# Two first expert tiles of a routed feed-forward layer moved in front of the loop and of the expert table

## Chip, cores and metric

The kernel runs on one core of one Trainium2 chip. The metric is device time in microseconds (us) of one execution. Engines are named as the profile names them: PE (TensorE), DVE (VectorE), ACT (ScalarE), POOL (GpSimd), SP (SyncE, which here only issues DMAs); PEld is the weight load of PE, and a name with a q at its end is the sequencer of that engine.

## What is computed

One transformer block on 1024 tokens of width 256: a normalised attention layer with 16 heads (softmax attention mixed with a linear-attention term), and then a feed-forward layer with 8 experts, of which each token takes its best 2. The second part is the one touched here:

```python
B, S, H, F, E, K = (2, 128, 256, 688, 8, 2)
logits = xf @ router_w.T
top_v, top_i = jax.lax.top_k(logits, K)
probs = jax.nn.softmax(top_v, axis=-1)
combine = jnp.sum(jax.nn.one_hot(top_i, E) * probs[..., None], axis=1)
g = jnp.einsum('th,efh->etf', xf, gate_w)
u = jnp.einsum('th,efh->etf', xf, up_w)
y = jnp.einsum('etf,ehf->eth', jax.nn.silu(g) * u, down_w)
out = jnp.einsum('te,eth->th', combine, y)
```

## The kernel before

Attention is worked off in 256 steps; work on the first half of the tokens (projection, norm, router, slots) is dealt out between its last steps. The experts are not computed for all tokens. Every token row, with its weight and number, is scattered to DRAM (`xg_d`, one list of rows for each expert): POOL does this with 8 indirect DMAs for each half of the tokens (`scatter`, L518 to L525; semaphore `scattered`). A tile is 128 rows of one list. The experts of the two first tiles (`EARLY = 2`) come from the counts of the first half alone (`early_ready`); those of all others from a table that DVE works out once the second half is routed (L975 to L1005, semaphore `expert_ready`, 2 at its end). The table also gives the number of pairs of tiles (`pairs`) and whether one is left over (`left`); each engine reads both into registers and runs a loop over pairs.

One tile t, with its buffers of parity t % 2, goes through these steps:

- SP: `load_xg` (L418) reads the row from a table into a register and brings 128 rows from `xg_d`.
- PE: `turn_x` (L1288) transposes the rows to bank 7 of PSUM; DVE: `xgT_copy` (L948) copies them and the two words of meta data.
- PE: `gate_up` (L1283), 16 matmul instructions to banks 0 to 3; ACT: `silu` (L646), reads banks 0 and 1; DVE: `hidden` (L1008), multiplies with banks 2 and 3.
- PE: `turn_hidden` (L1318), 6 transposes to banks 4 and 5; DVE: `hidT_copy` (L1014), two copies.
- PE: `down` (L1325), 12 matmul instructions to bank 6; ACT: `weigh` (L651), scales by the row's weight; POOL: `add_y` (L545), an indirect DMA that adds the rows to `sum_d`. DVE's `take_meta` (L1025) copies the meta data for `weigh` and `add_y`, and waits for the `add_y` of two tiles before.

In the loop body PE has the order: gate_up(t), turn_x for t+1, down(t-1), turn_hidden(t), gate_up(t+1), turn_x for t+2, down(t), turn_hidden(t+1), with t = 2i+1; this run has 20 tiles. Each engine takes its instructions in the order written; engines meet in semaphores alone.

Ahead of the loop, PE computes gate_up of tile 0 in pieces between the routing of the second half (L1309 to L1315). Then every engine waits for `expert_ready`, reads `pairs` and `left`, and only then goes on: DVE with `hidden(0, 0)`, PE with `turn_hidden(0, 0)` and the first pair of the loop (tiles 1 and 2), SP with the rows of tiles 2 and 3. SP waits for `scattered[1]` before `expert_ready`.

A load of a register from memory is `value_load`; on PE it is `load_expert` (L1272) for an expert's number. L1048 is the helper through which all matmuls pass, so a row of L1048 is told by its place and its count.

Of the kernel before, what the change touches and what calls it, by code (L numbers as in the profile page):

```python
# [13 lines left out]
P = 128  # L14
# [5 lines left out]
FB = [P, P, P, P, 88, 88]  # L20
FO = [sum(FB[:i]) for i in range(len(FB))]
FN = F // 2
NTILE = (K * T + E * (P - 1)) // P
EARLY = 2
PAIRS = (EARLY + NTILE - 1) // 2
# [47 lines left out]
def block_kernel(nc, x_d, w_d, rope_d, const_d, gate_d, router_d, gu_d, dn_d, out_d):  # L73
    ctx = ExitStack()
    with ctx:
# [120 lines left out]
        meta = keep(2, 2, dt=U32)  # L196
# [149 lines left out]
        def _(sp):  # L346
# [65 lines left out]
            def start_sum(hf):  # L412

                sp.wait_ge(x2_ready, 2 * hf + 2)
                sp.dma_start(sum_d[hf * HALF:(hf + 1) * HALF].rearrange("(n p) h -> p n h", p=P),
                             x[:, 4 * hf:4 * hf + 4]).then_inc(sum_init, 16)
# [11 lines left out]
            for t in range(EARLY):  # L428
                load_xg(t, t)
            start_sum(1)  # L430
            sp.wait_ge(scattered[1], 16 * K * 4)
            sp.wait_ge(expert_ready, 2)
            pairs = sp.value_load(pairs_i[0:1, 0:1], min_val=1, max_val=PAIRS)
            left = sp.value_load(pairs_i[0:1, 1:2], min_val=0, max_val=1)
            with sp.Fori(0, PAIRS) as i:
                with sp.If_lt(sp.to_reg(i), pairs):
                    for r in (1, 2):
                        t = 2 * i + r
                        sp.wait_ge(xgT_ready, t)
                        load_xg(t + 1, (r + 1) % 2)  # L440
# [7 lines left out]
        def _(pool):  # L448
# [93 lines left out]


            pool.wait_ge(sum_init, 48)
            def add_y(t, par):  # L545
                pool.wait_ge(y_added, 16 * t)
                pool.wait_ge(y_ready, t + 1)
                pool.sem_inc(y_taken, 1)
                pool.indirect_dma_start(  # L549
                    out=sum_d, out_offset=bass.IndirectOffsetOnAxis(ap=meta_y[:, par, 1:2], axis=0),  # L550
                    in_=yt[:, par], in_offset=None, compute_op=ALU.add).then_inc(y_added, 16)

            pool.wait_ge(expert_ready, 2)
            pairs = pool.value_load(pairs_i[0:1, 0:1], min_val=1, max_val=PAIRS)
            left = pool.value_load(pairs_i[0:1, 1:2], min_val=0, max_val=1)
            with pool.Fori(0, PAIRS) as i:
                with pool.If_lt(pool.to_reg(i), pairs):
                    for r in (0, 1):
                        add_y(2 * i + r, r)
# [6 lines left out]
        def _(act):  # L566
# [79 lines left out]
            def silu(t, par):  # L646
                act.wait_ge(gu_ps, t + 1)
                nc.scalar.activation(act_g[:, par].rearrange("p (b c) -> p b c", b=2),  # L648
                                     psum[:, 0:2, 0:FN], ACT.Silu).then_inc(silu_ready, 1)
# [5 lines left out]
                                     scale=meta_y[:, par, 0:1].bitcast(F32)).then_inc(y_ready, 1)  # L655

            silu(0, 0)
            act.wait_ge(expert_ready, 2)
            pairs = act.value_load(pairs_i[0:1, 0:1], min_val=1, max_val=PAIRS)
            left = act.value_load(pairs_i[0:1, 1:2], min_val=0, max_val=1)  # L660
            with act.Fori(0, PAIRS) as i:
                with act.If_lt(act.to_reg(i), pairs):
                    for r in (1, 2):
                        t = 2 * i + r
                        silu(t, r % 2)
                        act.wait_ge(y_added, 32 * i)
                        weigh(t - 1, (r + 1) % 2)
# [9 lines left out]
        def _(dve):  # L677
# [3 lines left out]
            def link(ins):  # L681

                chain[0] += 1
                ins.then_inc(dve_step, 1)
                dve.wait_ge(dve_step, chain[0])
# [230 lines left out]
            def steps(i, t):  # L916
# [8 lines left out]
                if isinstance(n, int) and n in SIDE:  # L925
# [19 lines left out]
                    if f == "early":  # L945
                        (early_counts, early_taken, early_experts)[k]()

            def xgT_copy(t, par):  # L948
                dve.wait_ge(xgT_ps, t + 1)
                V.tensor_copy(meta[:, par], xg[:, par, H:ROW].bitcast(U32))  # L950
                V.tensor_copy(xgT[:, par], psum[:, 7, 0:HB * P].rearrange("p (b c) -> p b c", b=HB)).then_inc(xgT_ready, 1)
# [12 lines left out]
            for k in range(K):  # L964
                for n in range(4):
# [7 lines left out]


            link(V.tensor_copy(cnt, psum[:, 4, 0:E]))  # L975
            link(V.tensor_tensor(cmp, cnt.unsqueeze(2).to_broadcast([P, E, E]),
                                 const[:, C_J:C_J + E * E].rearrange("p (e j) -> p e j", e=E), ALU.is_gt))
            link(V.tensor_reduce(tiles, cmp, AX.X, ALU.add))
# [15 lines left out]

            link(V.tensor_tensor(tau, cum.unsqueeze(1).to_broadcast([P, NTILE + 1, E]),
                                 const[:, C_TAU:].rearrange("p (n e) -> p n e", e=E), ALU.is_le))
            V.tensor_reduce(ex_f, tau, AX.X, ALU.add)
# [5 lines left out]
            V.tensor_scalar(row_i[:, EARLY:], ex_r, float(P), float(E * T), ALU.mult, ALU.min).then_inc(expert_ready, 1)  # L1005


            def hidden(t, par):  # L1008
                dve.wait_ge(silu_ready, t + 1)
                V.tensor_tensor(hid[:, par].rearrange("p (b c) -> p b c", b=2),  # L1010
                                act_g[:, par].rearrange("p (b c) -> p b c", b=2),
                                psum[:, 2:4, 0:FN], ALU.mult).then_inc(hid_ready, 1)

            def hidT_copy(t, par):  # L1014
                dve.wait_ge(hidT_ps, t + 1)
                V.tensor_copy(hidT[:, par, 0:4], psum[:, 4].rearrange("p (c t) -> p c t", c=4))  # L1016
                V.tensor_copy(hidT[0:FB[4], par, 4:6], psum[0:FB[4], 5, 0:2 * P].rearrange("p (c t) -> p c t", c=2)
                              ).then_inc(hidT_ready, 1)

            dve.wait_ge(expert_ready, 2)  # L1020
            pairs = dve.value_load(pairs_i[0:1, 0:1], min_val=1, max_val=PAIRS)
            left = dve.value_load(pairs_i[0:1, 1:2], min_val=0, max_val=1)
            hidden(0, 0)
            hidT_copy(0, 0)
            def take_meta(t, par):  # L1025

                dve.wait_ge(y_added, 16 * (t - 1))
                dve.wait_ge(xgT_ready, t + 1)
                V.tensor_copy(meta_y[:, par], meta[:, par])  # L1029

            with dve.Fori(0, PAIRS) as i:
                with dve.If_lt(dve.to_reg(i), pairs):
                    for r in (1, 2):
                        t = 2 * i + r
                        take_meta(t, r % 2)
                        xgT_copy(t + 1, (r + 1) % 2)
                        hidden(t, r % 2)
                        hidT_copy(t, r % 2)
# [7 lines left out]
        def _(pe):  # L1046
# [225 lines left out]
            def load_expert(t):  # L1272
                return pe.value_load(ex_i[0:1, bass.ts(t, 1)], min_val=0, max_val=E - 1)
# [9 lines left out]
            def gate_up(t, par, e):  # L1283
                pe.wait_ge(xgT_ready, t + 1)
                pe.wait_ge(hid_ready, t)
                columns(par, e, range(4)).then_inc(gu_ps, 1)

            def turn_x(par, loads):  # L1288
                pe.wait_ge(xg_in[par], 16 * loads)
                for b in range(HB):  # L1290
                    ins = nc.tensor.transpose(psum[:, 7, b * P:(b + 1) * P], xg[:, par, b * P:(b + 1) * P], ident)  # L1291
                ins.then_inc(xgT_ps, 1)
# [25 lines left out]
            def turn_hidden(t, par):  # L1318
                pe.wait_ge(hid_ready, t + 1)
                for c, (o, n) in enumerate(zip(FO, FB)):  # L1320
                    ins = nc.tensor.transpose(psum[0:n, 4 + c // 4, (c % 4) * P:(c % 4 + 1) * P],  # L1321
                                              hid[:, par, o:o + n], ident)
                ins.then_inc(hidT_ps, 1)

            def down(t, par, e):  # L1325
                pe.wait_ge(hidT_ready, t + 1)
                pe.wait_ge(y_ready, t)
                for c, n in enumerate(FB):
                    ins = mm(psum[:, 6, 0:H], hidT[0:n, par, c], dn[0:n, c, e], start=(c == 0),
                             stop=(c == len(FB) - 1))  # L1330
                ins.then_inc(y_ps, 1)

            pe.wait_ge(expert_ready, 2)
            pairs = pe.value_load(pairs_i[0:1, 0:1], min_val=1, max_val=PAIRS)
            left = pe.value_load(pairs_i[0:1, 1:2], min_val=0, max_val=1)
            turn_hidden(0, 0)
            pe.wait_ge(gu_in, 16 * E)
            pe.wait_ge(dn_in, 16 * len(FB))
            with pe.Fori(0, PAIRS) as i:
                with pe.If_lt(pe.to_reg(i), pairs):  # L1340

                    t = 2 * i + 1
                    e1 = load_expert(t)
                    gate_up(t, 1, e1)
                    turn_x(0, i + 2)
                    down(t - 1, 0, load_expert(t - 1))
                    e2 = load_expert(t + 1)
                    turn_hidden(t, 1)
                    gate_up(t + 1, 0, e2)
                    turn_x(1, i + 2)  # L1350
                    down(t, 1, e1)
                    turn_hidden(t + 1, 0)
# [35 lines left out]
```

## Time and profile before

| | us |
|---|---|
| median of 3 runs | 513.32 (511.92 to 514.02) |
| the profiled execution | 510.48 |
| its span in the trace | 508.6 |
| mean granted clock of PE | 0.927 |
| PE busy | 434.0 |
| DVE busy | 282.3 |
| ACT busy | 194.4 |
| POOL busy | 100.2 |

The first row of a timeline view gives: start in us from the beginning of the span, busy time, engine, line, operation, shapes, number of instructions, and in brackets the idle time before it with what ended it. The chain of waits follows the work that ended last backwards through what released it; "issue" in it is time in which nothing visible was waited for. [...] Ends of matmuls are modelled, so neighbouring rows can overlap by some tenths.

### The profile page before, as it was taken

The page shows a single profiled execution, that of the slowest core. Times are in us where ns is not written, and L with a number is a line of the kernel's source. Part 1 is how long each engine was busy: PE and PEld are TensorE (multiplying, and loading weights), DVE is VectorE, ACT ScalarE, POOL GpSimd, SP SyncE. Part 2 cuts the span into 40 slices and gives each one's busy share as a digit, 9 for nine tenths or more (in the row PEclk, how much of TensorE's full clock was granted, in tenths as well). Part 3 has the DMA queues.
Part 4 walks back from the last instruction along what each step waited for, and adds up shares of the span by engine and source line. Part 5 has one row for each costly group of instructions (what it writes and reads, how often), then busy time and mean ns, then how long its engine had stood idle before and what let it go on. Part 6 is the DMA issues. An engine that isn't in the chain of part 4 may idle for free.

```text
span 508.6 us, 7202 instructions
## 1 busy us (share of the span) xinstructions
PE 434.0 (85%) x2056; PEld 225.2 (44%) x2057; DVE 282.3 (56%) x511; ACT 194.4 (38%) x341; POOL 100.2 (20%) x91
## 2 busy tenths in 40 slices
PE   0990696898999999999998978589999999999981
PEld 0560263222222222424222335357777777777751
DVE  6577689587878887698884116512323323232310
ACT  1136410576676767575667941001111111110100
POOL 6252430111111110010060021602112121212111
PEclk9996597799999999999899997589999999999987
DMA  6137674194939361000021159412121212212004
GB/s 214 66 104 155 130 121 111 51 286 153 309 122 306 121 205 31 0 2 0 2 74 54 33 203 294 176 38 32 31 31 31 31 32 31 40 31 31 10 12 103
DMA packets 24452, 48.42 MB, mean 95 GB/s; under 512 B 4240, under 2 KB 17808, under 8 KB 22576
## 3 DMA queue, kind: packets, MB, share of 16 engines
q0 software_dynamic: 7824, 30.23, 20.7%
q1 hardware_dynamic: 16032, 16.35, 12.7%
q10 hardware_dynamic: 576, 1.58, 1.0%
q8 instruction: 11, 0.18, 0.2%
q14 instruction: 9, 0.07, 0.0%
HBM read 30.44 MB, written 18.70 MB: 97 GB/s over the span
## 4 chain that ended last, share of the span: by engine, by line
PE 66%; DVE 9%; DMA 9%; SPq 5%; issue 4%; ACT 3%; POOL 2%; POOLq 1%; DVEq 0%; ACTq 0%
PE psum L1048 61%; DMA mem<-parts_d 3%; DVE mem L755 3%; PE psum L1321 2%; DMA parts_d<-mem 2%; SPq L372 2%; ACT mem L628 2%; SPq L367 2%; DMA mem<-mem 1%; DMA mem<-x 1%; SPq L380 1%; PE psum L1291 1%; PE psum L1168 1%; DVE mem L845 1%; DMA xg_d<-mem 1%
## 5 line engine op out<-in xcount | busy, mean ns | idle before, releaser
L1048 PE MATMUL psum<-mem 128*32 128x512 f32 (+11 forms) x1800 | 406.7, 468 | 39.1 <-DMA mem<-parts_d 15.7
L1048 PEld LDWEIGHTS psum<-mem 128*128 128x128 f32 (+7 forms) x1800 | 192.6, 144 | 228.9 <-issue 98.1
L755 DVE TENSOR_REDUCE mem<-psum 128x1 f32<-128x1024 f32 x128 | 152.9, 1219 | 37.7 <-PE psum L1048 35.6
L628 ACT ACTIVATE mem<-psum 128x512 f32<-128x512 f32 x256 | 138.0, 605 | 88.8 <-PE psum L1048 86.1
L549 POOL DMA_INDIRECT sum_d<-mem x20 | 31.1, 1554 | 139.9 <-ACT mem L654 133.1
L648 ACT ACTIVATE mem<-psum 128x688 f32<-128x688 f32 x20 | 14.9, 743 | 107.9 <-PE psum L1048 107.9
L1029 DVE COPY mem<-mem 128x2 uint32<-128x2 uint32 x19 | 3.2, 169 | 62.8 <-DMA sum_d<-mem 62.8
L1016 DVE COPY mem<-psum 128x512 f32<-128x512 f32 x20 | 13.8, 692 | 38.7 <-PE psum L1321 37.1
L654 ACT ACTIVATE mem<-psum,mem 128x256 f32<-128x256 f32 x20 | 9.5, 473 | 48.3 <-PE psum L1048 48.3
L499 POOL DMA_DIRECT2D xg_d<-mem x9 | 8.1, 898 | 86.8 <-PE psum L1048 86.8
L1321 PE MATMUL psum<-mem 128*128 128x128 f32 (+1 forms) x120 | 17.3, 282 | 5.4 <-DVE mem L1010 5.4
L1010 DVE TENSOR_TENSOR mem<-mem,psum 128x688 f32<-128x688 f32 x20 | 17.4, 870 | 7.4 <-ACT mem L648 4.6
L1321 PEld LDWEIGHTS psum<-mem 128*128 128x128 f32 (+1 forms) x120 | 14.7, 141 | 8.6 <-DVE mem L1010 6.4
L523 POOL DMA_INDIRECT xg_d<-mem x16 | 15.8, 985 | 7.8 <-issue 4.2
L811 DVE RECIPROCAL mem<-psum 128x16 f32<-128x16 f32 x8 | 2.1, 258 | 26.9 <-PE psum L1168 26.7
L1055 PE MATMUL psum<-mem 128*128 128x128 f32 x16 | 3.9, 426 | 13.0 <-DVE mem L697 13.0
L459 POOL TENSOR_TENSOR mem<-mem 128x2 f32<-128x2 f32 (+1 forms) x6 | 5.2, 864 | 43.2 <-DVE mem L692 43.2
L484 POOL COPY mem<-mem 128x512 f32<-128x512 f32 x8 | 4.8, 611 | 39.9 <-PE psum L1048 39.9
L478 POOL TENSOR_TENSOR mem<-mem 128x2048 f32<-128x2048 f32 x2 | 9.0, 4507 | 13.8 <-ACT mem L598 7.9
L950 DVE COPY mem<-mem 128x2 uint32<-128x2 uint32 x20 | 3.4, 170 | 13.6 <-PE psum L1291 13.6
L469 POOL TENSOR_TENSOR mem<-mem 128x512 f32<-128x512 f32 x4 | 6.9, 1722 | 17.5 <-DVE mem L743 17.5
L731 DVE TENSOR_TENSOR mem<-mem 128x1024 bf16<-128x1024 f32 x4 | 7.1, 1774 | 4.4 <-ACT mem L587 4.4
(120 smaller groups left out, 191.6 us busy)
## 6 DMA issues: line engine op xcount, KB each, us to landing
mem<-gate_up POOLq DMA_DIRECT2D x8, 1376.0 KB, 8.4
xg_d<-mem POOLq DMA_DIRECT2D x8, 1032.0 KB, 6.8
mem<-down POOLq DMA_DIRECT2D x4, 1024.0 KB, 8.0
parts_d<-mem SPq DMA_DIRECT2D x12, 256.0 KB, 2.5
mem<-parts_d SPq DMA_DIRECT2D x24, 128.0 KB, 4.2
mem<-parts_d SPq DMA_DIRECT2D x48, 64.0 KB, 2.2
mem<-xg_d SPq DMA_DIRECT2D x20, 129.0 KB, 2.0
mem<-down POOLq DMA_DIRECT2D x2, 704.0 KB, 15.3
```

The lines of the kernel that those rows point to most:

```text
L367: sp.dma_start(kst[g * HD:(g + 1) * HD, qd], src).then_inc(done, 16)
L372: sp.dma_start(qst[g * HD:(g + 1) * HD, sl], src[:, :, cols(hf)]).then_inc(q_in, 16)
L523: pool.indirect_dma_start(out=xg_d, out_offset=bass.IndirectOffsetOnAxis(ap=slot[:, hf, k, n:n + 1], axis=0), in_=xn2[:, n, k], in_offset= ...
L549: pool.indirect_dma_start(out=sum_d, out_offset=bass.IndirectOffsetOnAxis(ap=meta_y[:, par, 1:2], axis=0), in_=yt[:, par], in_offset=None, ...
L628: nc.scalar.activation(prob[:, t % 8], psum[:, score_bank(n, t)], ACT.Exp, scale=HD ** -0.5).then_inc(exp_ready, 1)
L648: nc.scalar.activation(act_g[:, par].rearrange("p (b c) -> p b c", b=2), psum[:, 0:2, 0:FN], ACT.Silu).then_inc(silu_ready, 1)
L654: nc.scalar.activation(yt[:, par], psum[:, 6, 0:H], ACT.Copy, scale=meta_y[:, par, 0:1].bitcast(F32)).then_inc(y_ready, 1)
L755: V.tensor_reduce(mx[:, par, k:k + 1], banks(2 * (k % 2), 2), AX.X, ALU.max).then_inc(max_ready, 1)
L1010: V.tensor_tensor(hid[:, par].rearrange("p (b c) -> p b c", b=2), act_g[:, par].rearrange("p (b c) -> p b c", b=2), psum[:, 2:4, 0:FN], AL ...
L1016: V.tensor_copy(hidT[:, par, 0:4], psum[:, 4].rearrange("p (c t) -> p c t", c=4))
L1048: return nc.tensor.matmul(*a, **k)
L1321: ins = nc.tensor.transpose(psum[0:n, 4 + c // 4, (c % 4) * P:(c % 4 + 1) * P], hid[:, par, o:o + n], ident)
```

## The change

The pair of tiles 1 and 2 is written out in front of the loop, which now starts at pair 1, on every engine. Tiles 0 and 1 are finished without the table:

- DVE: `hidden(0, 0)` stands right behind the copy of the counts (L975), ahead of the table; `hidT_copy(0, 0)` in the middle of it (behind L992). `hidden`, `take_meta` and `hidT_copy` of tile 1 follow the table, and only then come the wait for it and the two register loads. The functions `hidden`, `hidT_copy` and `take_meta` are moved up as they are.
- PE: turn_hidden(0), gate_up(1), down(0), turn_hidden(1), down(1) come ahead of the wait for the table; then the loads of `pairs`, `left` and the third expert, turn_x for tile 2, gate_up(2), turn_x for tile 3, turn_hidden(2).
- ACT: both silu and both weigh ahead of the wait; silu(2) behind it.
- POOL: the two first add_y ahead of the wait.
- SP: waits for the table first and for `scattered[1]` second, issues the rows of tiles 2 and 3, and loads `pairs` and `left` after that.

```diff
             start_sum(1)
+            sp.wait_ge(expert_ready, 2)
             sp.wait_ge(scattered[1], 16 * K * 4)
-            sp.wait_ge(expert_ready, 2)
+            for t in range(EARLY):
+                sp.wait_ge(xgT_ready, t + 1)
+                load_xg(EARLY + t, t)
             pairs = sp.value_load(pairs_i[0:1, 0:1], min_val=1, max_val=PAIRS)
             left = sp.value_load(pairs_i[0:1, 1:2], min_val=0, max_val=1)
-            with sp.Fori(0, PAIRS) as i:
+            with sp.Fori(1, PAIRS) as i:
...
-            def add_y(t, par):
-                pool.wait_ge(y_added, 16 * t)
+            def add_y(t, par, first=False):
+                if not first:
+                    pool.wait_ge(y_added, 16 * t)
...
+            add_y(0, 0, first=True)
+            add_y(1, 1)
             pool.wait_ge(expert_ready, 2)
...
             silu(0, 0)
+            silu(1, 1)
+            weigh(0, 0)
+            weigh(1, 1)
             act.wait_ge(expert_ready, 2)
             pairs = act.value_load(pairs_i[0:1, 0:1], min_val=1, max_val=PAIRS)
             left = act.value_load(pairs_i[0:1, 1:2], min_val=0, max_val=1)
-            with act.Fori(0, PAIRS) as i:
+            silu(2, 0)
+            with act.Fori(1, PAIRS) as i:
...
             link(V.tensor_copy(cnt, psum[:, 4, 0:E]))
+            hidden(0, 0)
             link(V.tensor_tensor(cmp, cnt.unsqueeze(2).to_broadcast([P, E, E]),
...
+            hidT_copy(0, 0)
             link(V.tensor_tensor(tau, cum.unsqueeze(1).to_broadcast([P, NTILE + 1, E]),
...
+            hidden(1, 1)
+            take_meta(1, 1, first=True)
+            hidT_copy(1, 1)
             dve.wait_ge(expert_ready, 2)
             pairs = dve.value_load(pairs_i[0:1, 0:1], min_val=1, max_val=PAIRS)
             left = dve.value_load(pairs_i[0:1, 1:2], min_val=0, max_val=1)
-            hidden(0, 0)
-            hidT_copy(0, 0)
...
-            with dve.Fori(0, PAIRS) as i:
+            xgT_copy(2, 0)
+            take_meta(2, 0)
+            xgT_copy(3, 1)
+            hidden(2, 0)
+            hidT_copy(2, 0)
+            with dve.Fori(1, PAIRS) as i:
...
+            e1 = load_expert(1)
+            turn_hidden(0, 0)
+            gate_up(1, 1, e1)
+            pe.wait_ge(dn_in, 16 * len(FB))
+            down(0, 0, e0, first=True)
+            turn_hidden(1, 1)
+            down(1, 1, e1)
             pe.wait_ge(expert_ready, 2)
             pairs = pe.value_load(pairs_i[0:1, 0:1], min_val=1, max_val=PAIRS)
             left = pe.value_load(pairs_i[0:1, 1:2], min_val=0, max_val=1)
-            turn_hidden(0, 0)
+            e2 = load_expert(2)
+            turn_x(0, 2)
             pe.wait_ge(gu_in, 16 * E)
-            pe.wait_ge(dn_in, 16 * len(FB))
-            with pe.Fori(0, PAIRS) as i:
+            gate_up(2, 0, e2)
+            turn_x(1, 2)
+            turn_hidden(2, 0)
+            with pe.Fori(1, PAIRS) as i:
```

## Rows read from the trace of the kernel before

**Rows 1.** The page: PE's granted clock in 40 equal slices; shares of the chain.

```profile
PEclk9996597799999999999899997589999999999987
PE 66%; DVE 9%; DMA 9%; SPq 5%; issue 4%; ACT 3%; POOL 2%; POOLq 1%; DVEq 0%; ACTq 0%
```

**Rows 2.** Chain of waits, 323 to 360 us: start, duration, what.

```profile
328.99 3.26 DMA xg_d<-mem
332.27 0.27 SPq L433
...
334.52 1.96 DMA mem<-xg_d
...
355.74 0.22 PE psum L1291 x2
355.96 2.59 PE psum L1048 x12
358.55 0.66 PE psum L1321 x6
359.21 4.63 PE psum L1048 x16
```

**Rows 3.** Timeline of PE, 282 to 352 us (columns as told above).

```profile
313.35 7.76 PE L1048 MATMUL psum<-mem 128*128 128x8 f32 x40 [0.73 <-ACT mem L612]
326.55 1.54 PE L1321 MATMUL psum<-mem 128*128 128x128 f32 x6 [5.43 <-DVE mem L1010]
328.09 6.70 PE L1048 MATMUL psum<-mem 128*128 x16
336.53 0.44 PE L1291 MATMUL psum<-mem 128*128 128x128 f32 x2 [1.73 <-DMA mem<-xg_d]
337.51 4.44 PE L1048 MATMUL psum<-mem 128*128 x12 [0.55 <-issue]
...
350.85 1.42 PE L1048 MATMUL psum<-mem 128*128 x4
```

**Rows 4.** Timeline of DVE, ACT and POOL, 282 to 352 us.

```profile
319.55 0.16 DVE L975 COPY mem<-psum 128x8 f32<-128x8 f32 x1
...
323.66 0.18 DVE L1005 TENSOR_SCALAR mem<-mem 128x24 int32<-128x24 f32 x1
325.62 0.87 DVE L1010 TENSOR_TENSOR mem<-mem,psum 128x688 f32<-128x688 f32 x1 [1.78 <-issue]
...
337.08 0.42 DVE L951 COPY mem<-psum 128x256 f32<-128x256 f32 x1
...
342.75 0.69 DVE L1016 COPY mem<-psum 128x512 f32<-128x512 f32 x1 [4.47 <-PE psum L1321]
343.35 0.41 DVE L1017 COPY mem<-psum 88x256 f32<-88x256 f32 x1
347.19 0.17 DVE L1029 COPY mem<-mem 128x2 uint32<-128x2 uint32 x1 [3.43 <-DMA sum_d<-mem]
...
321.15 0.74 ACT L648 ACTIVATE mem<-psum 128x688 f32<-128x688 f32 x1 [3.06 <-PE psum L1048]
...
341.99 0.47 ACT L654 ACTIVATE mem<-psum,mem 128x256 f32<-128x256 f32 x1 [6.42 <-PE psum L1048]
```

**Rows 5.** PE over chosen stretches: us, busy (instructions), granted clock, DMA share, GB/s.

```profile
310.00:312.00 2.00, 0.47 (x4) 1.00 0.92 225
328.10:331.70 3.60, 3.60 (x7) 0.50 0.30 100
338.80:341.60 2.80, 2.80 (x8) 0.50 0.18 47
342.40:350.80 8.40, 8.40 (x39) 1.00 0.21 32
```

**Rows 6.** POOL's scatter of the second half, first and last of 8.

```profile
319.94 1.06 POOL L523 DMA_INDIRECT xg_d<-mem  x1 [3.30 <-DVE mem L892]
...
328.99 0.96 POOL L523 DMA_INDIRECT xg_d<-mem  x1 [0.30 <-issue]
```

More of the change, by code:

```diff
@@ L555, in _ @@
             left = pool.value_load(pairs_i[0:1, 1:2], min_val=0, max_val=1)
-            with pool.Fori(0, PAIRS) as i:
+            with pool.Fori(1, PAIRS) as i:
                 with pool.If_lt(pool.to_reg(i), pairs):
@@ L946, in steps, with hidden, hidT_copy, take_meta @@
                         (early_counts, early_taken, early_experts)[k]()
+            def hidden(t, par):
+                dve.wait_ge(silu_ready, t + 1)
+                V.tensor_tensor(hid[:, par].rearrange("p (b c) -> p b c", b=2),
+                                act_g[:, par].rearrange("p (b c) -> p b c", b=2),
+                                psum[:, 2:4, 0:FN], ALU.mult).then_inc(hid_ready, 1)
+            def hidT_copy(t, par):
+                dve.wait_ge(hidT_ps, t + 1)
+                V.tensor_copy(hidT[:, par, 0:4], psum[:, 4].rearrange("p (c t) -> p c t", c=4))
+                V.tensor_copy(hidT[0:FB[4], par, 4:6], psum[0:FB[4], 5, 0:2 * P].rearrange("p (c t) -> p c t", c=2)
+                              ).then_inc(hidT_ready, 1)
+            def take_meta(t, par, first=False):
+                if not first:
+                    dve.wait_ge(y_added, 16 * (t - 1))
+                dve.wait_ge(xgT_ready, t + 1)
+                V.tensor_copy(meta_y[:, par], meta[:, par])
             def xgT_copy(t, par):
@@ L1005, in _ @@
             V.tensor_scalar(row_i[:, EARLY:], ex_r, float(P), float(E * T), ALU.mult, ALU.min).then_inc(expert_ready, 1)
[L1008 to L1018, printed above, removed]
+            hidden(1, 1)
+            take_meta(1, 1, first=True)
+            hidT_copy(1, 1)
             dve.wait_ge(expert_ready, 2)
@@ L1022, in _ @@
             left = dve.value_load(pairs_i[0:1, 1:2], min_val=0, max_val=1)
-            hidden(0, 0)
-            hidT_copy(0, 0)
[L1025 to L1029, printed above, removed]
-            with dve.Fori(0, PAIRS) as i:
+            xgT_copy(2, 0)
[4 more added lines that the diff above has]
+            with dve.Fori(1, PAIRS) as i:
                 with dve.If_lt(dve.to_reg(i), pairs):
@@ L1323, in turn_hidden, with down @@
                 ins.then_inc(hidT_ps, 1)
-            def down(t, par, e):
+            def down(t, par, e, first=False):
                 pe.wait_ge(hidT_ready, t + 1)
-                pe.wait_ge(y_ready, t)
+                if not first:
+                    pe.wait_ge(y_ready, t)
                 for c, n in enumerate(FB):
```

## The prediction

> **What bounds the kernel now.** I read the page first. Its chain of waits is 66% PE, and the clock row has two dips of PE, one early and one shortly after the middle of the run, at slices 25 to 27 [rows 1]. That second dip is where the change works, so I then went through the chain from 320 us on, and beside it the timelines of all engines. From 350.85 us on PE has no gap: one tile takes 0.22 + 2.59 + 0.66 + 4.63 = 8.10 us, and matmul follows matmul [rows 2]. The stretch in front of it is different. PE ends its columns of tile 0 at 313.35 + 7.76 = 321.11 us, then stands for 5.43 us, works at half clock, stands for 1.73 us until the rows of tile 2 arrive, stands for 0.55 us for a register load, and only at 350.85 us begins the gate_up of tile 3 [rows 3]. Between 321.11 and 350.85 us lie 29.7 us, and the work in them (three turn_hidden, two gate_up, two turn_x, two down) costs at full clock 3 x 0.66 + 2 x 4.63 + 2 x 0.22 + 2 x 2.59 = 16.9 us. So 12.9 us are lost: 5.43 + 1.73 + 0.55 = 7.7 us idle and the rest, 5.2 us, mostly in the half clock.
>
> Why PE stands: `hidden(0, 0)` on DVE begins at 325.62, though its silu is over at 321.15 + 0.74 = 321.89 us. DVE is on the table until 323.84 and then spends 1.78 us on the wait and the two register loads [rows 4]. The chain itself runs elsewhere: over the last scatter (328.99 + 3.26 = 332.25 us), SP's registers and the rows of tile 2, which leave at 334.52 and are there at 336.48 us [rows 2]. Before, PE's first gap is therefore partly free: had PE been earlier with gate_up(1) alone, it would have waited longer for tile 2. The change moves both: the DVE work, and down(0), turn_hidden(1) and down(1) ahead of tile 2, so that PE has work while the scatter lands.
>
> **The new order, step by step,** in the times of the profiled execution; all up to 321.89 us stays.
>
> DVE waits behind the counts (319.55 + 0.16 = 319.71) for silu(0), which ends at 321.89. hidden(0) costs 0.87 and ends at 322.82 with the hand-over (0.06, as 325.62 + 0.87 = 326.49 against 326.55). Queued behind that wait is the table: it took 323.84 - 319.71 = 4.13 us, and with hidT_copy(0) in it (0.69 and 0.41 in a row, 343.76 - 342.75 = 1.01 us) it now ends at 322.82 + 4.13 + 1.01 = 327.96 instead of 323.84 us [rows 4]. Who waits for it: SP, which has to wait for the scatter till 332.25 anyway [rows 2], POOL and ACT, which take their first tiles ahead of it, and PE, not before 335. So 4.1 us of delay are free, with 4.3 us to spare; the cover is the scatter, and without it the table would cost its whole delay.
>
> PE: turn_hidden(0) from 322.88. At half clock it takes 1.54 us as before, to 324.42; gate_up(1) 6.70 us as before, to 331.12 [rows 3]. These two prices depend on when the clock returns. Before, it returned some 5.3 us after PE had restarted (half clock in 328.1 to 331.7, full from 332 on); in 338.8 to 341.6 the half clock lasted only about 3.4 us in all [rows 5]. With the same 5.3 us I take 6.70; the return 2 us earlier or 1.5 us later moves the end by 1.0 us down or 0.8 us up. down(0) needs hidT_copy(0), which lies inside a table that ends at 327.96, long before 331.12, and its weights, for which no wait shows before. It costs 2.59 [rows 2], to 333.71. Before, the same down took 4.44 us because the clock had fallen again [rows 3, 5]; here no gap precedes it. Meanwhile silu(1) 0.74 and hidden(1) 0.87 end at 331.12 + 0.74 + 0.87 + 0.1 = 332.83, so turn_hidden(1), 0.66, follows at once, to 334.37. hidT_copy(1), 1.05 with its hand-over, leaves PE idle to 335.45; that wait is new, since in the loop a gate_up covers it. down(1) 2.59, to 338.04.
>
> Behind down(1) in PE's sequencer stand three register loads. One left 0.55 us visible on PE [rows 3], two took 1.78 with the wait on DVE [rows 4]: three cost 1.65 to 2.67 us, beside a down of 2.59 us that also has to be issued. Exposed are 0 to 1.0 us; I take 0.35, nearer PE's own row. So turn_x(2) begins at 338.4. Its rows: SP now loads only the row's register after 332.25. Before, three loads and the loop's start took 334.52 - 332.27 = 2.25 us [rows 2]; one of three is some 0.75, so the DMA leaves at 333.0 and lands 1.96 later, at 335.0. That DMA moves 1.5 us forward and still counts for nothing: 3.4 us of slack. turn_x(2) 0.44, xgT_copy 0.42 and hand-overs (337.08 + 0.42 - 336.97 = 0.53 from the end of turn_x, [rows 3, 4]): gate_up(2) starts at 339.4 and ends at 344.0, turn_x(3) at 344.25. take_meta(2) waits for the first add_y: before, it came at 347.19, 4.73 us after weigh ended at 342.46 [rows 4]; now weigh(0) ends at about 334.3, so it is there at 339.0, before DVE wants it. The two register loads of DVE (1.78) lie between 336.5 and 338.3, under down(1).
>
> Then the price of peeling: turn_hidden(2) has no down in front of it as in the loop. silu 0.74 + hidden 0.87 + hand-overs put it at 345.8, an idle stretch of 1.5 us. It releases the sequencer too, which then enters the loop and loads a register before gate_up(3): before, this lasted from 326.55 to 328.09, 1.54 us [rows 3], against 0.66 of turn_hidden at full clock. So gate_up(3) starts at 347.35. Before it was 350.85 [rows 3]. **Sum: 350.85 - 347.35 = 3.5 us.** By parts: idle falls from 7.7 to 1.7 + 1.1 + 0.35 + 0.5 + 1.5 + 0.9 = 6.05 us, 1.65 less, and the fall of the clock around down(0) goes, 4.44 - 2.59 = 1.85 us. After it loop, skipped turns and tail are the same, each shifted by this; add_y takes 4.7 us a tile against 8.1 us of PE, so it doesn't bind. Below these bounds nothing: no work is taken out but one wait.
>
> POOL's issues of the scatter were 1.06 us beside the table and 0.96 us without [rows 6]. More copies of DVE now run beside them; eight times 0.1 is 0.8 us at most, under the slack of 3.4 us. [...]
>
> **The rivals.**
> A, the sum above: -3.5 us.
> B, the clock falls once more. PE's new gaps of 1.5 and 0.9 us at 344.25 to 347.35, with 0.7 us of work between, resemble the 1.73 and 0.55 us after which the clock fell before [rows 3, 5]; speaking against it, a gap of 1.5 us (PE busy 0.47 of 2.00) at 310 us left the clock at 1.00 [rows 5]. Price: as for down(0), 1.85 us, so -1.65 us, 511.7. [...]
> C, the clock is back earlier than before: gate_up(1) at 4.63 instead of 6.70 us. PE then stands only 1.7 us instead of 5.43 before turn_hidden(0), which speaks for it; that it was at half clock already before that gap speaks against it [rows 1]. -5.5 us, 507.8.
> D, the transfers are the bound: the change moves nothing of the scatter, and if tile 2 lands later than 338.4 the gain shrinks by the excess. It would take 3.4 us more of scatter; from 6.9 us more nothing is left. At 5 us of delay: -1.9 us, 511.4.
> E, slower: the short gaps at 334.4, 338.0 and 344.3 us each cost a fall of the clock, so PE never runs warm till the loop. Three times 1.85 is 5.55 us, from the second on the gain is about gone (-3.5 + 3.7): +2.05 us, 515.4.
>
> **How the numbers follow.** The profiled execution took 510.48 us, 1.9 more than its span; the sum makes it 507.0. The median of the runs shown is 513.32, and even the lowest is 1.4 above the profiled one. The difference of the two kernels is what I work out, so it goes off the median: 513.32 - 3.5 = 509.8. Chances: A 0.58, B 0.19, C 0.12, D 0.04, E 0.07. A's own range, with gate_up(1) -1.0 to +0.8, the registers -0.35 to +0.65 and 0.7 us of scatter between medians (511.92 to 514.02 for single runs), is 507.8 to 511.9. To leave out no more than 2 in 10 it must take in B and most of C: 507.3 to 512.4. A measurement of this kernel can tell about 0.5%, 2.6 us, from no change; that bound is at 510.75. C and most of A lie below it, B, D and the weak end of A within: faster 0.65, same 0.30, slower 0.05.
>
> **What would show it.** In the profile after: hidden(0) at about 321.95 and PE's gap ahead of turn_hidden(0) 1.7 us; the table's end at 328; down(0) right behind gate_up(1), 12 instructions in 2.6 us; a gap of about 1.1 us before down(1); rows of tile 2 landed at 335, and no wait of turn_x(2) for a DMA; gaps of 1.5 and 0.9 us around turn_hidden(2); the gate_up of tile 3, 16 instructions, from 347.35. Wrong would be: turn_x(2) waiting for the DMA (D), PEclk of 0.5 after 345 (B) or 1.00 already at 325 (C), a stretch at 0.50 behind each gap (E), or a tail longer than before, which no step above foresees.

## The result, and the profile after

The changed kernel takes 507.36 us at the median of 20 runs, the kernel before 513.27 at the median of 20. The ratio is 0.9883 with a 95% interval of 0.9858 to 0.9909: 6.0 us faster (4.7 to 7.3), where 3.5 were forecast. Two more measurements of the same pair gave 0.9908 (0.9882 to 0.9934) and 0.9900 (0.9865 to 0.9935). The forecast of 509.8 us was 2.4 us too slow, and the first ratio stands at the very end of the range (513.32 x 0.9883 = 507.3).

The profiled execution of the changed kernel took 508.72 us, its span is 506.9 (508.6 before), mean granted clock 0.932 as a share of full speed (so 1.00 is full and 0.50 half clock in what follows; PEclk on the page is in tenths). The page has its second dip of the clock at slices 25 to 27 like [rows 1], but shallower, and it reaches into slice 28:

```profile
PEclk9996587599999999999998998788999999999997
PE 67%; DVE 11%; DMA 7%; SPq 5%; issue 4%; ACT 3%; POOL 1%; POOLq 0%; DVEq 0%; ACTq 0%
```

The timeline of PE from 290 to 352 us answers to [rows 3]. L1067 is the helper of the matmuls, L1340 turn_hidden, L1310 turn_x; in each variant below these lines have other numbers by a few, so tell a row by its place and its count:

```profile
314.88 8.00 PE L1067 MATMUL psum<-mem 128*128 128x8 f32 x40 [0.73 <-ACT mem L618]
324.69 0.87 PE L1340 MATMUL psum<-mem 128*128 128x128 f32 x6 [1.81 <-DVE mem L960]
325.40 7.38 PE L1067 MATMUL psum<-mem 128*128 x28
332.72 0.88 PE L1340 MATMUL psum<-mem 128*128 128x128 f32 x6
335.18 4.54 PE L1067 MATMUL psum<-mem 128*128 x12 [1.59 <-DVE mem L967]
339.56 0.38 PE L1310 MATMUL psum<-mem 128*128 128x128 f32 x2
340.68 4.89 PE L1067 MATMUL psum<-mem 128*128 x16 [0.74 <-issue]
...
347.31 0.87 PE L1340 MATMUL psum<-mem 128*128 128x128 f32 x6 [1.52 <-DVE mem L960]
348.78 3.90 PE L1067 MATMUL psum<-mem 128*128 x7 [0.60 <-issue]
```

The order is the one forecast: a gap of 1.81 us instead of 5.43, gate_up(1) and down(0) in one row of 28 instructions, the new waits ahead of down(1) and turn_hidden(2). One thing is not: turn_hidden(0) takes 0.87 us and not 1.54, and the 28 instructions take 7.38 us and not 6.70 + 2.59 = 9.29. PE is at full clock here (1.00 in 322 to 335 us). In this execution part of that is lost again, since the clock falls in down(1) (0.50 in 336 to 339 us, 4.54 us for 12 instructions).

This execution reached the end of tile 0's columns 1.8 us later than that of before (322.88 against 321.11), from what came earlier, which the change doesn't touch. So the fair measure is the stretch from there to the gate_up of tile 3: 348.78 - 322.88 = 25.9 us, before 29.7. Behind it both are equally long: 506.9 - 348.8 = 158.1 us, before 157.8. That is partly chance in this trace: the first gate_up of the loop runs at half clock for a while (0.50 in 349.4 to 352.6 us, 6.58 us in all instead of 4.89), and in return the fall of the clock that the kernel before has near its end (0.50 in 486 to 488 us) is missing.

### The profile page after: what moved, and what is told of

Its sections match the earlier page's. It is cut to its first block, busy times and chain, and to the rows that moved or that the text cites. A ratio compares the mean times of both kernels' runs of the same rounds, so it can differ in the third digit from the quotient of the medians.

```text
span 506.9 us, 7154 instructions
## 1 busy us (share of the span) xinstructions
PE 434.5 (86%) x2056; PEld 226.3 (45%) x2057; DVE 282.0 (56%) x511; ACT 194.8 (38%) x341; POOL 100.2 (20%) x91
## 4 chain that ended last, share of the span: by engine, by line
PE 67%; DVE 11%; DMA 7%; SPq 5%; issue 4%; ACT 3%; POOL 1%; POOLq 0%; DVEq 0%; ACTq 0%
PE psum L1067 62%; DVE mem L765 4%; DMA mem<-parts_d 3%; PE psum L1340 3%; DMA parts_d<-mem 2%; SPq L372 2%; ACT mem L634 2%; SPq L367 2%; DMA mem<-x 1%; PE psum L1187 1%; PE psum L1310 1%; DVE mem L855 1%; DVE mem L738 1%; POOL mem L462 1%; DVE mem L741 0%
## 5 line engine op out<-in xcount | busy, mean ns | idle before, releaser
L1067 PE MATMUL psum<-mem 128*32 128x512 f32 (+11 forms) x1800 | 407.6, 469 | 39.9 <-DMA mem<-parts_d 15.2
L1067 PEld LDWEIGHTS psum<-mem 128*128 128x128 f32 (+7 forms) x1800 | 194.2, 144 | 229.7 <-issue 99.9
L975 DVE COPY mem<-mem 128x2 uint32<-128x2 uint32 x19 | 3.2, 168 | 55.8 <-DMA sum_d<-mem 55.7
L1340 PE MATMUL psum<-mem 128*128 128x128 f32 (+1 forms) x120 | 16.6, 274 | 3.3 <-DVE mem L960 3.3
L1340 PEld LDWEIGHTS psum<-mem 128*128 128x128 f32 (+1 forms) x120 | 13.8, 135 | 6.2 <-DVE mem L960 4.5
L481 POOL TENSOR_TENSOR mem<-mem 128x2048 f32<-128x2048 f32 x2 | 9.0, 4508 | 13.3 <-ACT mem L604 7.9
```

The source lines that it names most:

```text
L1067: return nc.tensor.matmul(*a, **k)
```

## The experiments

Each was timed in rounds against the kernel before on the same chip; "stretch" is the time from the end of tile 0's columns to the gate_up of tile 3 in its own trace.

**The kernel before, again (before_again).** No edit.

> The kernel before, unchanged, timed against itself, to see how far its executions spread and where the granted clock of PE falls in another execution. Theory 'clock' (the new order by itself is worth the 3.5 to 3.8 us of the sum, and the other 2 us of the measured 5.9 come from fewer falls of PE's clock on average): ratio 1.00 within 0.3%; the half-clock stretches around 325 to 342 us and at the tail (485 us) sit elsewhere or are missing in this profile, and the span from the end of the columns of tile 0 to the gate_up of tile 3 differs from 29.7 us by up to 2 us. Theory 'size' (a step of the sum is mis-sized, the clock is the same on average): that span is 29.7 us within 0.3 us again.

Measured: 0.9992 (0.997 to 1.0013); stretch 30.3 us. Mean granted clock over 25 executions of the kernel before 0.9305. The clock around the stretch, as views of PE over windows (us, busy, granted clock, DMA share, GB/s):

```profile
318.00:322.00 4.00, 3.98 (x22) 0.50 0.96 341
322.50:325.50 3.00, 0.00 (x0) 1.00 0.35 128
326.00:332.40 6.40, 4.97 (x12) 0.50 0.30 105
```

Here the clock had come back at 322.3 us, while PE stood in its gap of 5.43 us, and was gone again when turn_hidden(0) began at 327.41. In the first trace it was at half clock all through the gap. To PE it makes no difference: in both traces gate_up(1) begins at half clock behind this gap. Neither theory got what it asked for: the half-clock stretches sit where they sat (gate_up(1) 6.64, down(0) 4.54 us), against 'clock', and the stretch differs from 29.7 by 0.6 us, against 'size'.

**The changed kernel, again (after_again).** No edit.

> The changed kernel again. Both theories: ratio 0.988 within 0.003 to the kernel before. Theory 'clock': mean granted clock over its executions is 0.008 to 0.015 above that of the kernel before (2 us lost less are 4 us less at half clock, and 17 us fewer in the stretch around the two first tiles), and the span from the end of the columns of tile 0 to the gate_up of tile 3 varies by 1 us or more between this profile and the first (25.9 us). Theory 'size': that span is 25.9 us within 0.3 us again, and the mean clocks differ by under 0.004.

Measured: 0.9908 (0.9882 to 0.9934); mean clock 0.942 over 6 executions (0.940 over the 20 of the first measurement): 0.010 to 0.012 above the kernel before, as theory 'clock' had it. Stretch 25.2 us, 0.7 from the first: between the two theories.

```profile
312.00:318.00 6.00, 6.00 (x36) 0.50 0.51 147
318.50:322.00 3.50, 1.69 (x11) 1.00 0.68 283
322.00:331.00 9.00, 7.97 (x35) 1.00 0.30 105
```

The clock comes back ahead of the gap, and it is still at 1.00 behind the 1.81 us of idle. Something new stands in the chain of waits:

```profile
328.29 2.86 DMA xg_d<-mem
...
331.92 3.37 DMA mem<-xg_d
335.29 0.04 issue
335.33 0.44 PE psum L1310 x2
```

PE, now early, waits 1.29 us for the rows of tile 2, and their load takes 3.37 us where it took 1.96 [rows 2]. POOL had issued the first add_y 1.27 us before this load:

```profile
330.65 1.62 POOL L553 DMA_INDIRECT sum_d<-mem  x1 [1.39 <-issue]
```

**SP's part alone (sp_first).** The kernel before with:

```diff
+            sp.wait_ge(expert_ready, 2)
             sp.wait_ge(scattered[1], 16 * K * 4)
-            sp.wait_ge(expert_ready, 2)
+            for t in range(EARLY):
+                sp.wait_ge(xgT_ready, t + 1)
+                load_xg(EARLY + t, t)
...
-            with sp.Fori(0, PAIRS) as i:
+            with sp.Fori(1, PAIRS) as i:
```

> The kernel before with SP's part of the change alone: the rows of tiles 2 and 3 leave before pairs and left are loaded. Theory 'clock': they land 1.5 us earlier, PE's gap before turn_x(2) shrinks from 1.73 to about 0.2 us, and with a gap that short the clock does not fall in down(0): -1.5 us, or -3.3 us where the fall would have come. Rival 'all needed together' (nothing of the change is worth anything while the first hidden waits for the table): 0 within 0.5 us. From my sum: -1.5 to -3.3 us.

Measured: 0.9955 (0.9934 to 0.9977), 2.3 us faster; stretch 26.6 us, 3.4 less than the mean of the three traces of before.

```profile
328.21 6.47 PE L1051 MATMUL psum<-mem 128*128 x16
335.22 0.44 PE L1294 MATMUL psum<-mem 128*128 128x128 f32 x2 [0.54 <-DMA mem<-xg_d]
336.21 2.85 PE L1051 MATMUL psum<-mem 128*128 x12 [0.55 <-issue]
```

The load left 0.8 us after the scatter had landed instead of 2.25, so 1.5 us sooner; the wait is 0.54 instead of 1.73 us, and down(0) keeps its clock (1.00 in 332 to 340 us): 2.85 against 4.44 us [rows 2, 3]. In the trace this is worth more than the 1.5 us, since down(0), behind the shorter wait, keeps its clock; the measured gain, 1.2 to 3.4 us by its interval, doesn't decide between 1.5 us alone and the two together.

**Down(1) behind gate_up(2) (order2).** The changed kernel with:

```diff
-            down(1, 1, e1)
             pe.wait_ge(expert_ready, 2)
...
             gate_up(2, 0, e2)
             turn_x(1, 2)
+            down(1, 1, e1)
             turn_hidden(2, 0)
```

and weigh(1) behind silu(2), DVE's register loads ahead of hidden(1).

> The changed kernel with down(1) moved behind gate_up(2) and turn_x(3), as in the loop (weigh(1) behind silu(2), and DVE's two register loads ahead of hidden(1)). If the peeled order costs what the sum says (1.1 us idle before down(1), 0.35 of register loads, 1.5 idle before turn_hidden(2) and 0.9 behind it, less a wait of about 1.1 us for tile 2's rows and their copy), the gate_up of tile 3 starts 3.1 us earlier than in the changed kernel: -3.1 us to it, -9 us to the kernel before (ratio 0.982). Rival: the new gap of 1.7 us at 334.4 makes the clock fall in gate_up(2), which costs 1.9 us: -1.2 us to the changed kernel.

Measured: 0.9945 (0.9923 to 0.9966), some 2 us slower than the changed kernel, where 3.1 faster was expected; stretch 28.2 us.

```profile
331.32 0.82 PE L1340 MATMUL psum<-mem 128*128 128x128 f32 x6
337.49 0.69 PE L1310 MATMUL psum<-mem 128*128 128x128 f32 x2 [5.36 <-DMA mem<-xg_d]
338.92 7.53 PE L1067 MATMUL psum<-mem 128*128 x16 [0.74 <-issue]
```

PE is done with turn_hidden(1) 10.6 us after the columns (the sum had 13.3), the rows come at 15.9, and with nothing in between the gap grows to 5.36 us and gate_up(2) runs at half clock (0.50 in 334.2 to 344 us), as the rival had it, but behind a gap three times as long. The two errors of the sum, clock and landing, show here at their full size. It also tells what down(1) ahead of tile 2 is good for: it fills the time until the rows land.

**The first add_y held back (late_add, late_add_2).** The changed kernel with:

```diff
+            pool.wait_ge(xg_in[0], 32)
+            pool.wait_ge(xg_in[1], 32)
             add_y(0, 0, first=True)
```

> The changed kernel, but POOL waits for the rows of tiles 2 and 3 before it issues the first add_y. In the three traces of kernels with the change, the load of tile 2's rows took 3.3 to 3.4 us from issue to landing where an add_y had been issued 1.3 us before it, against 2.0 us in the three traces without the change. Theory 'collision' (the add_y that the change moves forward slows the load of tile 2): the load takes 2.0 us, turn_x(2) starts 1.3 us earlier than in the second profile of the changed kernel, and the gate_up of tile 3 starts 24.0 us after the end of tile 0's columns instead of 25.2: -1.2 us to the changed kernel, ratio 0.987 to the kernel before. Rival 'cold queue' (the load is slow because it follows the scatter sooner): still 3.3 us, no change.

Measured: 0.9885 (0.9849 to 0.9921), stretch 24.1 us, 503.67 us at the median; the lines of the chain:

```profile
332.95 1.99 DMA mem<-xg_d
...
334.99 0.44 PE psum L1312 x2
```

and POOL's first add_y, now behind the loads:

```profile
336.99 1.62 POOL L553 DMA_INDIRECT sum_d<-mem  x1 [7.20 <-DMA mem<-xg_d]
```

> The changed kernel with the first add_y held back, again, since its first interval (0.985 to 0.992) holds that of the changed kernel. Theory 'collision': the load of tile 2's rows 2.0 us again, the gate_up of tile 3 24.0 to 24.2 us after the end of tile 0's columns against 25.0 to 25.9 in the three traces of the changed kernel, and a ratio of 0.985 to 0.989, below the 0.990 of the changed kernel. Rival: what is won before the loop is given back behind it (the clock falls there instead): span saved 1.2 us in front, nothing in total, 0.990.

Measured: 0.9884 (0.9844 to 0.9924), load 2.0 us, stretch 23.8 us, 503.49 us. The load is back at 2.0 us, so it was the add_y issued 1.3 us ahead of it that slowed it. (The expectation speaks of three traces with a slow load; in the first trace of the changed kernel the add_y came at 335.22, with the load at 335.30, and the load took 1.9 us. The slow ones, 3.37 and 3.36, were after_again and order2; after_third adds 3.02.) The stretch, 23.95 us in the mean of the two traces, is 1.4 us shorter than the mean of the changed kernel and 1.2 shorter than in the two traces of it without a fall of the clock in the stretch, as expected. That the whole is faster than the changed kernel isn't shown: the ratios are 0.9885 and 0.9884 against 0.9883, 0.9908 and 0.9900, and medians of different measurements can't be set side by side, since the kernel before itself stood at 513.27 in one and at 509.79 to 510.59 in the others. In both traces the part behind the stretch is shorter too, 156.5 and 156.7 us against 157.9 to 158.1, because they have no fall of the clock behind the stretch while PE works (after_again and after_third have one at 479 and 480 us, the first trace one at 349); whether that follows from the edit or is chance stays open.

**Hidden first alone (hid_first).** The kernel before with `hidden(0, 0)` behind the counts, `hidT_copy(0, 0)` in the table, and on PE:

```diff
+            turn_hidden(0, 0)
             pe.wait_ge(expert_ready, 2)
             pairs = pe.value_load(pairs_i[0:1, 0:1], min_val=1, max_val=PAIRS)
             left = pe.value_load(pairs_i[0:1, 1:2], min_val=0, max_val=1)
-            turn_hidden(0, 0)
```

> The kernel before with hidden(0) and hidT_copy(0) ahead of and inside the table, and PE's turn_hidden(0) ahead of its wait for the table, all else as before. Theory 'clock' (a gap of 5.4 us on PE makes the clock fall again, one of 1.8 us does not): turn_hidden(0) runs at full clock in 0.87 us, but PE then stands 5.5 us or more for the table (4.2 us later than before) and its registers, gate_up(1) starts 2 us later than before and at half clock, and ends after tile 2's rows are there: +1 us (0 to +2). Rival 'hidden first is the gain': -1 us or better.

Measured: 0.9969 (0.994 to 0.9997); stretch 29.4 us. It was to be slower by 1 us and is not: 1.6 us faster (0.2 to 3.1), the number that the rival 'hidden first is the gain' had named, though the interval all but touches no change and the stretch is only 0.6 us under the mean of before.

```profile
323.29 0.87 PE L1321 MATMUL psum<-mem 128*128 128x128 f32 x6 [1.81 <-DVE mem L950]
331.07 6.30 PE L1048 MATMUL psum<-mem 128*128 x16 [6.91 <-issue]
338.19 0.44 PE L1291 MATMUL psum<-mem 128*128 128x128 f32 x2 [0.82 <-DMA mem<-xg_d]
339.18 2.85 PE L1048 MATMUL psum<-mem 128*128 x12 [0.55 <-issue]
```

The first half went as told: full clock behind 1.81 us (1.00 in 323 to 325 us), half clock behind 6.91 us (0.50 in 328 to 333 us). What I had not reckoned is that a later gate_up(1) ends only 0.82 us before the rows, and that the clock stays in down(0) (1.00 in 334 to 345 us, 2.85 us for the 12 instructions).

**SP's part undone (sp_undone).** The changed kernel with SP as before.

> The changed kernel with SP as before (pairs and left loaded ahead of the rows of tile 2). The rows leave 1.4 us later. By my sum they would still be there in time (336.5 against 338.4): 0 us to the changed kernel. By the traces since, PE is at full clock from tile 0's turn_hidden on and waits for these rows: +1.4 us to the changed kernel, less what of the collision with the first add_y goes, so 0 to +1.4 us, ratio about 0.992 to the kernel before.

Measured: 0.9944 (0.9915 to 0.9972), in the middle some 2 us slower than the changed kernel, though the intervals overlap; stretch 25.8 us. The load took 2.16 us, issued 3.1 us behind the add_y and out of its way; PE waited 1.93 us for it. In this trace the clock also fell behind 345 us (0.50 in 346 to 349 us, gate_up of tile 3 in 6.58 us). By the sum it should have cost nothing; the wait of 1.93 us shows that the slack of 3.4 us that I gave this load did not exist.

**PE's gap filled (before_fill).** The kernel before with 10 useless matmuls in the gap of 5.43 us (each call of `mm` here is two instructions in a trace, as 8 calls make the 16 of gate_up):

```diff
             columns(0, e0, (3,)).then_inc(gu_ps, 1)
+            pe.wait_ge(xgT_ready, 2)
+            for k in range(5):
+                for b in range(HB):
+                    mm(psum[:, 7, 0:FN], xgT[:, 0, b], gu[:, 0, b, 0:FN], start=(b == 0), stop=(b == HB - 1))
```

> The kernel before with 10 useless matmul instructions of 344 columns into the free bank 7 in PE's gap of 5.4 us between tile 0's last columns and turn_hidden(0). Theory 'clock': the clock stays up or is back, turn_hidden(0) takes 0.87 and gate_up(1) 4.7 us instead of 1.54 and 6.7; yet tile 2's rows come when they come, PE stands 2.7 us longer for them, and the time is that of the kernel before within 0.3%: in the kernel before the half clock in gate_up(1) was covered by the scatter. Rival 'the half clock in gate_up(1) was on the path': -2.7 us, ratio 0.995.

Measured: 1.0021 (0.9994 to 1.0049).

```profile
327.03 0.87 PE L1325 MATMUL psum<-mem 128*128 128x128 f32 x6 [0.66 <-DVE mem L1010]
328.71 4.89 PE L1048 MATMUL psum<-mem 128*128 x16 [0.81 <-issue]
337.15 0.69 PE L1291 MATMUL psum<-mem 128*128 128x128 f32 x2 [3.56 <-DMA mem<-xg_d]
338.14 5.40 PE L1048 MATMUL psum<-mem 128*128 x12 [0.30 <-issue]
```

Nothing was changed but PE's idle time, and turn_hidden(0) takes 0.87 and gate_up(1) 4.89 us. The granted clock is back at 319.4 us, ahead of the fillers, and stays at 1.00 through the fillers, where in before_again it came back and went in the idle gap. So here it was the idle gap that cost the clock. Nothing is won all the same: PE stands 3.56 us for the rows instead of 1.73 (2.7 more were expected, 1.8 came), which takes all that gate_up(1) won, and the clock falls in this wait (at 336.5 us, 0.50 to 343), so that down(0) takes 5.40 us instead of 4.44. In the kernel before, the half clock of gate_up(1) was covered by the scatter; in the changed kernel down(0) stands directly behind gate_up(1), and the same clock lies on the path.

**A third trace of each (before_third, after_third).** No edit.

> The kernel before once more, for a third trace. Theory 'clock' (PE's gap of 5.4 us ahead of turn_hidden(0) makes or keeps the half clock, so gate_up(1) begins at half clock in every execution): turn_hidden(0) 1.5 us, gate_up(1) over 6 us, and again a fall in down(0) or behind it; from the end of tile 0's columns to the gate_up of tile 3 29.7 to 30.3 us. Rival 'chance' (the half clock there came by chance in the two first traces): turn_hidden(0) 0.87 us and gate_up(1) 4.9 us in this one.

Measured: 1.002 (0.9995 to 1.0044); turn_hidden(0) 1.54, gate_up(1) 5.88, down(0) 4.13 us; stretch 30.05 us. "Over 6 us" was missed by little, since the clock came back sooner behind PE's restart: at 329.3 us, 3.6 us behind it, where the first trace had 5.2. As in before_again, it had stood at 1.00 in the gap (320 to 322 us) and was gone before turn_hidden(0) (0.50 in 323 to 325 us).

> The changed kernel once more, for a third trace. Theory 'clock': turn_hidden(0) at 0.87 us and gate_up(1) with down(0) in 7.4 us, as in all traces with the change so far; the same span 25.2 to 25.9 us; ratio 0.988 to 0.991. Theory 'collision': the load of tile 2's rows takes 3.3 us again. Where PE's clock falls later (behind 330 us, at the tail) differs from the first two traces: one had falls at 336 and 349 us, the other at 479 us.

Measured: 0.99 (0.9865 to 0.9935); turn_hidden(0) 0.88, the 28 instructions 7.38 us, load of tile 2 3.02 us, stretch 25.0 us; its clock falls again only at 480 us.

**Later gaps filled as well (late_fill).** The kernel with the add_y held back, with 4 useless matmuls (8 instructions in the trace) before down(1) and 4 before turn_hidden(2):

```diff
             turn_hidden(1, 1)
+            keep_busy(7, 2)
             down(1, 1, e1)
...
             turn_x(1, 2)
+            pe.wait_ge(y_ready, 2)
+            keep_busy(6, 2)
             turn_hidden(2, 0)
```

> The changed kernel with the first add_y held back as in the run before, and with useless matmuls (4 instructions of 344 columns each time, into a bank that is free) in PE's gaps of 1.2 us before down(1) and of 1.5 us before turn_hidden(2). If falls of the clock behind these gaps (seen in 1 of 2 traces of the changed kernel, and in the one with SP's part undone) cost 1.5 to 1.9 us each time: 0.8 us faster on average than with the add_y held back alone, ratio 0.987, and no stretch at half clock between 322 and 355 us. Rival: the fillers run over the end of the gaps and cost 0.2 to 0.4 us, no fall is saved: ratio 0.989 to 0.990.

Measured: 0.9899 (0.9867 to 0.9932); no half clock between 322 and 355 us, but none was there without the fillers either in two traces; stretch 24.6 us, 0.5 to 0.8 more than in the two traces of late_add. The fillers run over: the second set takes 2.48 us in a gap of 1.52. The ratio is the one the rival named; the intervals are too wide to tell it from 0.9885, but nothing of the 0.8 us gain shows.

## Why the forecast was too small

The marks of the sum against the traces, in us from the end of tile 0's columns:

| mark | forecast | after | after_again | late_add |
|---|---|---|---|---|
| turn_hidden(0) | 1.8 | 1.8 | 1.8 | 1.8 |
| gate_up(1) | 3.3 | 2.5 | 2.5 | 2.5 |
| turn_hidden(1) | 12.6 | 9.8 | 9.7 | 9.8 |
| down(1) | 14.3 | 12.3 | 11.8 | 11.8 |
| turn_x(2) | 17.3 | 16.7 | 15.9 | 14.8 |
| gate_up(2) | 18.3 | 17.8 | 17.1 | 16.0 |
| turn_hidden(2) | 24.7 | 24.4 | 23.7 | 22.6 |
| gate_up(3) | 26.2 | 25.9 | 25.2 | 24.1 |

**The clock at the start: the mis-sized term.** "With the same 5.3 us I take 6.70", and 1.54 for turn_hidden(0). turn_hidden(0) measured 0.7 from start to start, and gate_up(1) with down(0) 7.22 in after_again, where the sum had 9.29, so the step was too dear by 0.8 + 2.1 = 2.9 us. I had carried over the price of work behind a gap of 5.43 us to a place behind a gap of 1.8 us. The reason given against the rival, that PE was at half clock already before the gap, was true of the row and misled: half clock ahead of the gap says nothing on whether it would have come back with work coming on. before_fill shows the gap as the cause, and all nine traces with hidden(0) moved (turn_hidden(0) 0.87 or 0.88 us) against four without it or a filler (1.54 us) agree. This was rival C, at 0.12 too low a chance; its mechanism came in every trace, its time (-5.5) almost.

Where falls come later differs between traces of the same kernel: the changed kernel's clock fell at 336 and 349 us in one trace, at 479 in another, at 480 in the third. Behind the gaps of 1.52 us before turn_hidden(2) and of 0.55 to 0.60 us after it, the clock fell in the first trace and in sp_undone, and stayed at 1.00 in after_again, after_third, late_add and late_add_2; what decides it no run shows. At the start of the stretch no chance shows: gate_up(1) began at half clock in all four traces with 5.43 to 5.97 us of idle ahead of turn_hidden(0), and ran at full clock in all eight with 1.81 us there and turn_hidden(0) directly ahead of it.

**The rows of tile 2: a slack that wasn't there.** The step put turn_x(2) at 338.4 with rows at 335.0. Counted from the end of the columns that is 17.3 and 13.9. PE is ready at 14.6 us, and the rows come at 15.9 with the collision and at 14.8 without. Three parts: PE came early, for the reason above; the add_y that the change moves forward slows the load by 1.0 to 1.4 us where it is issued 1.3 to 1.4 us ahead; and the last scatter landed 11.7 us after the columns in after_again and 12.0 in late_add, where the sum had 11.1 from the first trace. This last part isn't of the change: the kernel before has 11.1, 11.6 and 11.9 in its three traces. I had costed that add_y for when it ends, not for what it does to the transfer beside it. Rival D asked for 3.4 us more of scatter; a wait of 1.1 to 1.3 us came with 0.6 to 0.8. By luck this error hid part of the other: -2.9 and +1.3, with the small ones below, make the sum only 1.0 us too slow in after_again.

**What held.** PE's gap 1.81 (1.7 forecast); the end of the table 6.6 us after the columns (6.85), covered as told; the wait before down(1) 1.22 (1.1), but for 1.59 in the first trace; before turn_hidden(2) 1.52 (1.5); from there to gate_up(3) 1.47 (1.54). Register loads behind down(1): nothing exposed in late_add_2, where turn_x(2) follows at once, against 0.35. From turn_x(2) to gate_up(2) 1.18, against 0.97. The fall in down(0), 1.85, was before's and is gone. The scatter's issues stayed at 0.96 to 1.07 us but for one of 1.14. That DVE's work beside them costs the 0.1 us that I gave it isn't shown: in after_again the first issue, at 319.25, took 1.07 us while DVE stood (319.02 to 320.29 us), and those at 323.23 and 324.50 took 0.96 us with DVE busy beside them.

**Rival B** came in the first trace of the changed kernel: it fell in down(1) and again behind the written-out tile 2 (4.54 and, in the first gate_up of the loop, 6.58 us), not in the other two. E never came.

**The total.** The three stretches of before are 29.7, 30.3 and 30.05, mean 30.0; of the changed kernel 25.9, 25.2 and 25.0, mean 25.4: 4.7 us. The three ratios give 6.0, 4.7 and 5.1 us. The spans of the same six traces differ by 4.6 us in the mean (508.9 and 504.3), so in the traces the stretch is the whole gain, and it lies within the intervals of two of the three ratios and at the edge of the first; whether the 0.6 us between the means (5.3 and 4.7) is chance, or falls of the clock elsewhere, stays open. Of the 4.7, the sum had 3.5; 0.3 of the rest is that before's own trace was its shortest.

How the parts share it can be read only roughly: SP's part alone is worth 2.3 us (1.2 to 3.4), hidden first alone 1.6 (0.2 to 3.1), and undoing SP's part in the changed kernel costs some 2, with overlapping intervals. The down(0) and down(1) ahead of tile 2 were not tried alone.

## What to carry to other kernels

Before a row's duration is carried to another place, look at what stood ahead of it: the same 16 matmul instructions took 5.9 to 6.7 us behind a gap of 5.4 to 6.0 us and 4.9 us where PE had work. Here idle time of PE had a second price behind it, so shortening a wait can pay twice, though only where the work behind it is on the path: a transfer that left 1.5 us sooner into such a gap paid 2.3 (1.2 to 3.4), and useless matmuls that kept the clock in front of the same transfer paid nothing (ratio 1.0021). And when a step is moved forward, ask of each DMA of it which other transfer it now meets: here two waits that hold the first add_y back took 1.2 to 1.4 us off the stretch, while a gain in the total isn't shown.

## What the runs showed of the hardware

PE's clock came back once while PE stood: in before_again it was granted 1.00 from 322.3 to 325.7 us with no matmul, and was at 0.50 again before work began; before_third (1.00 in 320 to 322 us, 0.50 from 323) and sp_first (1.00 in 322 to 324 us, 0.50 from 325) show that a clock at 1.00 when PE stopped was lost in such a gap too (5.97 and 5.43 us idle). And the load of tile 2's rows, 129 KB from DRAM, took 1.9 to 2.1 us with no indirect add issued ahead of it and 3.0 to 3.4 us when an indirect add into another DRAM tensor had been issued 1.3 to 1.4 us before; issued 3.1 us behind the add, it took 2.2, and issued 0.1 us behind it, in the first trace of the changed kernel, 1.9 (the load of tile 3's rows behind it took 2.3).
